# Moving the expert-weight loads of a transformer layer to the last two pairs of each attention step

## The chip, the core and the metric

The kernel runs on one core of a Trainium2 chip. The metric is the device time of one execution in microseconds (us). TensorE (PE) multiplies, VectorE (DVE) and ScalarE (ACT) do element-wise work, GpSimd (POOL) does some of it too and issues DMAs through the software queue, SyncE (SP) only issues DMAs through a hardware queue. Every DMA, whoever issues it, runs on the same 16 DMA engines.

## The reference

The input is 32 sequences of 256 tokens, 128 features each, all in float32. Each token is normalised, and the layer adds three things: the token, an attention block with its own MLP, and a mixture of 9 experts of which every token takes 2.

```python
x = L0_attn_hidden_states
xn = _layernorm(x, axis=-1)
x = x + _L0_attn_ref(xn, ...) + _L0_ffn_ref(xn, Wr, Wg, Wu, Wd)

# attention: 16 heads of 8, causal
attn = softmax(where(causal, Q K^T * scale, -1e9));  ctx = attn @ V
h = xn + ctx @ out_U @ out_V + out_b
h + gelu(_layernorm(h) @ fc1_U @ fc1_V + fc1_b) @ fc2_U @ fc2_V + fc2_b

# experts: E = 9, two per token, inner width 352
hidden = silu(xf @ Wg[e]) * (xf @ Wu[e]);  out = sum over e of cw[t, e] * hidden @ Wd[e]
```

## The kernel before, in words

Engines run their own written-out programs and meet at semaphores. The work has four stages: layer norm and routing scores, attention (from about 93 to 612 us), the experts, and the MLP. The change lies in attention alone.

Attention goes over 16 chunks of 512 tokens, one step per chunk, two sequences per chunk. A step has 24 slots, 12 for each sequence. In each slot PE makes one block of scores (`score_unit`, lines L1022 and L1023), ACT takes its exponential (L817), and PE multiplies by V two slots later. Interleaved with it runs a second pass that is 8 slots or more ahead: `max_unit` (L999, L1002) makes the scores for the row maxima, DVE takes the maxima (L1393), PE turns them (L1053), ACT negates them (`copy_max`, L810), and SP copies the resulting 16x256 numbers, 16 KB, as one more row into the stacked queries with a DMA (`stack_max`, L474). This row is called **the maxima row** here. The score block of slot 0 and that of slot 12 wait for it (`max_stacked`), since the exponential must be taken of scores less their maximum. The row for a step's first sequence is issued near slot 21 of the step before, the row for its second sequence near slot 9.

SP also copies the projected queries into the stack (`stack_q`, L451), 12 DMAs of 32 KB per sequence, the first of them at a step's start and after slot 12. POOL copies the keys (`stack_k_part`, L609, 128 KB each), scatters token rows to their expert slots (`scatter`, L652, 64 KB each), and loads the expert weights (`load_weights`, L600 and L604).

POOL walks a step in 12 **pairs** of slots. At the head of pair k it waits until 2k+1 score blocks of the step are done. Then it issues what the tables put there: scatters at pairs 0 to 8 in steps 3 to 10 (at all 12 pairs in steps 11 to 14), key copies for the next chunk's second sequence at pairs 1, 2 and 3, the bias at pair 7, key copies for the chunk after it at pairs 8, 9 and 10. The zero fills of the slot buffer (`fill`, L589, 516 KB each) are at pairs 0 to 7 in steps 0 and 1, with one more in step 2.

The weights come in 15 loads in steps 3 to 10. Their order is, for each group of three experts, Wg, Wu (528 KB each), then three parts of Wd (192, 192 and 144 KB). They are waited for only in the last step (`experts_loaded`). Before the change a step issues its two loads at pair 0 and pair 6. Within a pair the load is the last thing that POOL issues.

Step 3 begins at about 207 us in the trace and a step takes some 31 to 33 us.

Of the kernel before, what the change touches and what calls it, by code (L numbers as in the profile page):

```python
# [63 lines left out]
def layer_kernel(nc, x_in, w, out):  # L64
# [28 lines left out]
    with whole:  # L93
        ident = keep("ident", [P, P])
        wq = keep("wq", [P, P])
        wk = keep("wk", [P, P])
        wv = keep("wv", [P, P])
        wo = keep("wo", [P, P])
        w1 = keep("w1", [P, HID])
        w2 = keep("w2", [P, HCH, P])  # L100
        q_bias = keep("q_bias", [P, 1])
        k_bias = keep("k_bias", [P, 1])
        v_bias = keep("v_bias", [P, P])
        mlp_bias = keep("mlp_bias", [P, HCH])
        out_bias = keep("out_bias", [P, P])
        fc2_bias = keep("fc2_bias", [P, P])
        with nc.sbuf_tensor("first_words", [P, EXPERTS * (2 * FF + len(FF_CHUNKS) * P)], F32) as first_words:
            pass
        w_gate_up = keep("w_gate_up", [P, EXPERTS, 2 * FF], F32R)
        w_down = keep("w_down", [P, EXPERTS, len(FF_CHUNKS), P])  # L110

        even_stack = keep("even_stack", [P, GROUPS * LANES * CHUNK], F32R)
        assert EXPERTS * 2 * FF <= GROUPS * LANES * CHUNK
        w_hi = even_stack[:, 0:EXPERTS * 2 * FF].rearrange("p (e f) -> p e f", e=EXPERTS)
        mix = keep("mix", [P, tiles, 2])
        slot_of = keep("slot_of", [P, tiles * 2], U32)
        tile_expert = keep("tile_expert", [1, slot_tiles], I32)
        ln2_stats = keep("ln2_stats", [P, tiles * 6])

        first_and_attention(nc, locals())  # L120
        experts_and_mlp(nc, locals())
# [34 lines left out]
def first_and_attention(nc, env):  # L156
# [13 lines left out]
    UNITS = 12  # L170
# [4 lines left out]
    with ExitStack() as stack:  # L175
# [171 lines left out]
        LATE = 3  # L347
        W_STEPS, LAST_ROWS = 8, 8
# [4 lines left out]
        def when(j):  # L353

            step = max(k for k, n in ROWS_AT.items() if n <= j)
            return step, j - ROWS_AT[step]

        XS_AT = {(LATE - 1, 1): 0, (LATE - 1, 2): 1}
        for c in range(2, chunks):
            step, row = when(2 * TPC * (c - 1) - 1)  # L360
# [19 lines left out]

        def weights_at(step, pair):

            if pair in W_AT and LATE <= step < LATE + W_STEPS:
                k = 2 * (step - LATE) + W_AT.index(pair)
                return k if k < W_LOADS else None
            return None

        K_SECOND_AT, K_FIRST_AT, BIAS_AT, W_AT = (1, 2, 3), (8, 9, 10), 7, (0, 6)

        MAX_FROM = 8  # L390
        EARLY = 2 * UNITS - MAX_FROM
# [16 lines left out]
        with nc.Block() as block:  # L408
# [140 lines left out]
            def _(pool):  # L549
# [109 lines left out]
                def step(half, d):  # L659
                    p = at(half, d)  # L660
                    x = p.index
                    last = x == last_chunk
                    two_ahead = x < last_chunk - 1
                    for pair in range(HALVES):
                        after_scores(p, 2 * pair + 1)
                        rows, blank_part, weights = scatter_at(x, pair), fill_at(x, pair), weights_at(x, pair)
                        if x == LATE and pair == 0:
                            pool.wait_ge(slots_ready, 1)
                            pool.wait_ge(zero_filled, 16 * FILLS)
                            pool.wait_ge(routed_all, 1)  # L670
                        if rows is not None:
                            if rows[1] == 0:
                                number_rows(at(0, rows[0]))
                            scatter(at(0, rows[0]), rows[1])
                        if blank_part is not None:
                            fill(blank_part)
                        if pair == BIAS_AT:
                            add_bias(p)
                        if pair in K_SECOND_AT and not last:
                            stack_k_part(at(half, d + 1), 1, K_SECOND_AT.index(pair))  # L680
                        if pair in K_FIRST_AT and two_ahead:
                            if pair == K_FIRST_AT[0]:
                                pool.wait_ge(k_split, x + 3)
                                pool.sem_inc(k_stack_started, 1)
                            stack_k_part(at(half, d + 2), 0, K_FIRST_AT.index(pair))
                        if weights is not None:
                            load_weights(weights)
# [1357 lines left out]
```

## Time and profile before

| | us |
|---|---|
| median of 3 runs | 1030.56 |
| lowest, highest | 1028.12, 1031.29 |
| the profiled execution | 1028.12 |
| its span, first to last instruction | 1026.4 |
| PE busy | 966.4 (94%) |
| DVE busy | 703.0 (68%) |
| ACT busy | 538.1 (52%) |
| POOL busy | 431.6 (42%) |

The span is what the trace covers; 1.7 us lie around it. TensorE's granted clock over the whole run is 0.960 of full speed, and 1.00 in the attention steps 3 to 15. PE is busy nearly all of the attention stage.

### The profile page before, as it was taken

Reading aid. Unit: us, or ns where it says so; the run is one execution under the profiler, and the core shown is the slowest. Engines: PE = TensorE matmul, PEld = TensorE weight load, DVE = VectorE, ACT = ScalarE, POOL = GpSimd, SP = SyncE. Lnnn points to the kernel's source line nnn. Section 1 sums busy time; section 2 is a strip of 40 time slices with the busy share of each in tenths; the row PEclk is TensorE's granted clock in tenths of the full one; section 3 lists DMA queues with packets and bytes.
Section 4 is the critical chain, followed back from the end, with each engine's and each line's share of the span. In section 5 each row is a group of like instructions: output and inputs, shape, how many; then the busy total and the mean of one; then the engine's idle time right before and its main releaser. Section 6 shows DMA issues by size and latency. Waiting matters only on the chain. (4 is left out here: it accounts for less than half of the span.)

```text
span 1026.4 us, 25266 instructions
## 1 busy us (share of the span) xinstructions
PE 966.4 (94%) x7701; PEld 750.1 (73%) x7701; DVE 703.0 (68%) x3192; ACT 538.1 (52%) x1256; POOL 431.6 (42%) x563
## 2 busy tenths in 40 slices
PE   3768999999999999999999987999999999999997
PEld 3435565666666666666666647999999999999896
DVE  4758488877778777787777763555555554558887
ACT  1653255554555555555555574555555555564442
POOL 9462122154544545445555522545445444441110
PEclk9666699999999999999999998999999999999999
DMA  8285355355445455343433204222222222238784
GB/s 234 87 228 177 111 176 185 107 153 127 124 132 154 136 140 143 98 137 114 142 110 117 83 31 121 63 66 63 64 66 69 68 66 61 74 98 252 210 234 134
DMA packets 133558, 127.13 MB, mean 124 GB/s; under 512 B 17274, under 2 KB 113652, under 8 KB 133428
## 3 DMA queue, kind: packets, MB, share of 16 engines
q1 hardware_dynamic: 109860, 67.83, 24.2%
q0 software_dynamic: 20592, 56.43, 17.5%
q10 hardware_dynamic: 2976, 1.26, 0.5%
q8 instruction: 67, 1.10, 0.5%
q14 instruction: 63, 0.52, 0.2%
HBM read 57.15 MB, written 42.60 MB: 97 GB/s over the span
## 5 line engine op out<-in xcount | busy, mean ns | idle before, releaser
L1393 DVE CUSTOM_DVE_ANT_0 att_masked_st<-att_m_ps,att_mask_st 128x128 bf16<-128x128 f32 (+1 forms) x1024 | 313.0, 353 | 109.8 <-PE att_m_ps L999 78.8
L817 ACT ACTIVATE att_probs<-att_t_ps 128x512 f32<-128x512 f32 x384 | 229.4, 598 | 213.2 <-PE att_t_ps L1023 208.6
L1641 POOL DMA_INDIRECT y_scratch<-moe_y,moe_row_now x136 | 132.3, 972 | 151.9 <-DVE moe_y L1895 110.4
L652 POOL DMA_INDIRECT slot_x<-att_xs,att_slot_now x128 | 126.9, 991 | 160.7 <-PE att_t_ps L1023 138.0
L1889 DVE TENSOR_TENSOR moe_hidden<-moe_gate,moe_up_ps 128x352 f32<-128x352 f32 x136 | 70.9, 521 | 113.7 <-ACT moe_gate L1816 110.2
L1023 PE MATMUL att_t_ps<-att_mask_ts,att_ident_b 128*128 128x256 bf16 (+1 forms) x384 | 124.6, 324 | 0.0
L1718 PE MATMUL moe_y_ps<-w_down,moe_hidden_t 128*128 (+1 forms) x816 | 113.8, 275 | 1.3 <-DVE moe_y L1895 1.2
L1816 ACT ACTIVATE moe_gate<-moe_gate_ps 128x352 f32<-128x352 f32 x136 | 63.1, 464 | 96.2 <-PE moe_up_ps L1701 96.2
L1718 PEld LDWEIGHTS moe_y_ps<-w_down,moe_hidden_t 128*128 128x128 f32 (+1 forms) x816 | 101.8, 191 | 2.4 <-issue 2.3
L1393 DVE DVE_READ_ACCUMULATOR2_ANT att_row_max<- 128x1 f32 x1024 | 84.6, 83 | 0.0
L1022 PE MATMUL att_t_ps<-att_odd_stack,att_k_stack 97*128 97x512 f32 x192 | 81.0, 423 | 3.1 <-DMA att_odd_stack<-att_neg_max 2.7
L1022 PE MATMUL att_t_ps<-even_stack,att_k_stack 97*128 97x512 f32 x192 | 82.0, 427 | 1.5 <-DMA even_stack<-att_neg_max 1.3
L1038 PE MATMUL att_pv_ps<-att_probs,att_v_ones 128*32 128x256 f32 x1024 | 82.7, 395 | 0.0
L1023 PEld LDWEIGHTS att_t_ps<-att_mask_ts,att_ident_b 128*128 128x128 bf16 x384 | 37.7, 98 | 61.4 <-issue 49.3
L609 POOL DMA_DIRECT2D att_k_stack<-att_qk_parts x96 | 55.2, 576 | 48.3 <-PE att_t_ps L1023 45.5
L999 PE MATMUL att_m_ps<-att_k_stack,even_stack 96*128 96x256 f32 x256 | 70.6, 359 | 2.4 <-DVE att_row_max L1393 2.3
L999 PE MATMUL att_m_ps<-att_k_stack,att_odd_stack 96*128 96x256 f32 x256 | 68.6, 350 | 0.0
L1710 PE MATMUL moe_hidden_ps<-ident,moe_hidden 128*128 128x128 f32 (+1 forms) x408 | 66.9, 273 | 0.0
L999 PEld LDWEIGHTS att_m_ps<-att_k_stack,even_stack 96*128 96x128 f32 x256 | 42.4, 203 | 22.9 <-issue 18.1
L1701 PE MATMUL moe_gate_ps<-even_stack,moe_x_lo 128*128 x136 | 55.8, 411 | 0.6 <-DVE moe_x_lo L1883 0.6
L999 PEld LDWEIGHTS att_m_ps<-att_k_stack,att_odd_stack 96*128 96x128 f32 x256 | 40.7, 194 | 20.4 <-issue 18.9
L1810 ACT CAST moe_x_hi<-moe_x_ps 128x128 fp32r<-128x128 f32 x136 | 36.2, 266 | 34.0 <-PE moe_x_ps L1682 32.4
(264 smaller groups left out, 2072.9 us busy)
## 6 DMA issues: line engine op xcount, KB each, us to landing
att_k_stack<-att_qk_parts POOLq DMA_DIRECT2D x96, 128.0 KB, 3.2
slot_x<-att_xs POOLq DMA_DIRECT2D x17, 516.0 KB, 3.3
moe_x<-slot_x SPq DMA_DIRECT2D x34, 258.0 KB, 2.8
att_xs<-xn_scratch SPq DMA_DIRECT2D x32, 256.0 KB
mlp_rows<-y_scratch POOLq DMA_DIRECT2D x16, 512.0 KB, 5.4
even_stack<-att_qk_parts SPq DMA_DIRECT2D x192, 32.0 KB
att_odd_stack<-att_qk_parts SPq DMA_DIRECT2D x192, 32.0 KB
xn_scratch<-att_probs POOLq DMA_DIRECT2D x16, 256.0 KB, 3.0
```

Source lines behind the costliest of these rows:

```text
L652: pool.indirect_dma_start(env["slot_x"][:], bass.IndirectOffsetOnAxis(ap=slot_now[c.parity][:, col:col + 1], axis=0), xs[c.parity][:, t, k ...
L817: act.activation(probs[:, m % PT, :], t_ps[m % 2][:], ACT.Exp).then_inc(exp_done, 1)
L999: last = pe.matmul(ps[:, n * SEQ:(n + 1) * SEQ], q[0:ROWS, g, i, hi:hi + P], k[0:ROWS, g, lo:lo + SEQ], start=True, stop=True)
L1022: pe.matmul(by_lane, keys, q[rows, g, lanes, queries], start=True, stop=False, skip_group_check=True)
L1023: pe.matmul(by_lane[:, :, 0:P], ident_b[:], mask_ts[:, lanes, :], start=False, stop=True, skip_group_check=True).then_inc(scores_done, 1)
L1038: last = pe.matmul(pv_ps[b][32 * i:32 * i + 32, at_col:at_col + SEQ], v_ones[c.parity][:, 2 * b, head_of(u, i), :], pt, start=(u == 0), st ...
L1393: last = dve.tensor_tensor_reduce(out=masked_st[m % 2][:, part], in0=m_ps[m % 2][:, part], in1=mask_st[:, SEQ - width:], scale=1.0, scalar ...
L1641: pool.indirect_dma_start(env["y_dram"][:], bass.IndirectOffsetOnAxis(ap=row_now[q.parity][:, t:t + 1], axis=0), y[c.parity][:], None).the ...
L1710: last = pe.transpose(hidden_ps[0:n, k * P:(k + 1) * P], hidden[c.parity][:, col:col + n], ident[:])
L1718: last = pe.matmul(y_ps[:, 0:P], hidden_t[c.parity][0:n, k * P:(k + 1) * P], down_cols[0:n, ds(e * (NCH * P) + k * P, P)], start=(k == 0), ...
L1816: act.activation(gate[c.parity][:], gate_ps[c.parity][:, 0:FF], ACT.Silu).then_inc(gate_done, 1)
L1889: dve.tensor_tensor(hidden[c.parity][:], gate[c.parity][:], up_ps[c.parity][:, 0:FF], ALU.mult).then_inc(hidden_done, 1)
```

## The change

The two weight loads of a step leave pairs 0 and 6 and go to pairs 10 and 11, the last two. Which load belongs to which step stays as it was.

```diff
         def weights_at(step, pair):
 
-            if pair in W_AT and LATE <= step < LATE + W_STEPS:
-                k = 2 * (step - LATE) + W_AT.index(pair)
+            if pair >= UNITS - 2 and LATE <= step < LATE + W_STEPS:
+                k = 2 * (step - LATE) + pair - (UNITS - 2)
                 return k if k < W_LOADS else None
             return None
 
-        K_SECOND_AT, K_FIRST_AT, BIAS_AT, W_AT = (1, 2, 3), (8, 9, 10), 7, (0, 6)
+        K_SECOND_AT, K_FIRST_AT, BIAS_AT = (1, 2, 3), (8, 9, 10), 7
```

`UNITS` is 12, `LATE` is 3, `W_STEPS` is 8 and `W_LOADS` is 15. The programs of PE, DVE, ACT and SP are the same, row for row; only POOL's changes.

POOL at pair 6 to pair 10 of step 3, before. The names: `att_scores_done` is the wait at a pair's head, L652 are scatters, L609 key copies.

```order
L652 DMA slot_x<-att_xs0,att_slot_now0 17408x129 [waits att_scores_done] x3
L600 DMA w_gate_up<-in_L0_ffn_Wu 128x3x352
L652 DMA slot_x<-att_xs0,att_slot_now0 17408x129 [waits att_scores_done]
L637 TENSOR_TENSOR att_xn_both<-att_xn_both,out_bias 128x512 [waits att_xn_loaded1]
L643 COPY att_slot_now1<-slot_of 128x8 [waits att_scores_done]
L644 COPY att_xs1<-att_row_of 128x8
L652 DMA slot_x<-att_xs1,att_slot_now1 17408x129 [waits att_xs_loaded1,att_slot_ready]
L609 DMA att_k_stack1<-att_qk_parts 32x4x256 [waits att_k_split]
L609 DMA att_k_stack1<-att_qk_parts 32x4x256 [waits att_scores_done] x2
L652 DMA slot_x<-att_xs1,att_slot_now1 17408x129 [waits att_scores_done]
L604 DMA w_down<-in_L0_ffn_Wd 128x3x128
```

The Wu load stands at pair 6, ahead of pair 7's scatter; the last two rows are pair 0 of step 4, with the next load.

POOL at pairs 4 to 11 of step 3 and the start of step 4, after.

```order
L652 DMA slot_x<-att_xs0,att_slot_now0 17408x129 [waits att_scores_done] x4
L637 TENSOR_TENSOR att_xn_both<-att_xn_both,out_bias 128x512 [waits att_xn_loaded1]
L643 COPY att_slot_now1<-slot_of 128x8 [waits att_scores_done]
L644 COPY att_xs1<-att_row_of 128x8
L652 DMA slot_x<-att_xs1,att_slot_now1 17408x129 [waits att_xs_loaded1,att_slot_ready]
L609 DMA att_k_stack1<-att_qk_parts 32x4x256 [waits att_k_split]
L609 DMA att_k_stack1<-att_qk_parts 32x4x256 [waits att_scores_done] x2
L600 DMA w_gate_up<-in_L0_ffn_Wg 128x3x352
L600 DMA w_gate_up<-in_L0_ffn_Wu 128x3x352 [waits att_scores_done]
L652 DMA slot_x<-att_xs1,att_slot_now1 17408x129 [waits att_scores_done] x2
L609 DMA att_k_stack1<-att_qk_parts 32x4x256
```

Both loads of the step now stand between the third key copy of pair 10 and the scatter of the next step's pair 0: Wg directly behind that key copy, Wu behind the wait of pair 11.

SP around the same boundary, the same before and after.

```order
L451 DMA att_odd_stack<-att_qk_parts 8x4x256 [waits att_scores_done,att_q_split]
L451 DMA att_odd_stack<-att_qk_parts 8x4x256 x11
L474 DMA even_stack<-att_neg_max 1x16x256 [waits att_max_copied]
L451 DMA att_odd_stack<-att_qk_parts 8x4x256 [waits att_scores_done,att_q_split]
L451 DMA att_odd_stack<-att_qk_parts 8x4x256 x11
```

Nothing moved here; the maxima row (L474) of the next step's first sequence stands between two groups of query copies.

## Rows read from the trace of the kernel before

**Rows 1.** Waits of PE, 205 to 460 us: us in total, times, longest us.

```profile
PE att_t_ps L1022 <- DMA even_stack<-att_neg_max: 1.1, 3, 0.7
PE att_t_ps L1022 <- DMA att_odd_stack<-att_neg_max: 0.6, 2, 0.4
```

**Rows 2.** Windows, steps 3 to 10: us, busy us per engine, PEclk, DMA share, GB/s.

```profile
207.60:460.30 252.70, 250.92 (x2211) 162.19 (x2209) 195.03 (x1138) 142.04 (x256) 124.60 (x161) 1.00 0.49 134
```

**Rows 3.** Timeline of SP and PE, end of step 5: start us, us, instruction.

```profile
300.78 0.55 SPq L474 DMA_DIRECT2D even_stack<-att_neg_max  x1
...
302.71 0.50 PE L999 MATMUL att_m_ps<-att_k_stack,even_stack 96*128 96x256 f32 x2
303.05 0.40 PE L1022 MATMUL att_t_ps<-even_stack,att_k_stack 97*128 97x512 f32 x1
```

**Rows 4.** Line L474, all 32: issue start to landing, min/median/max us.

```profile
DMA to landing us min/median/max: 2.1/2.1/3.3
```

**Rows 5.** DMA view, 301.90 to 302.30 us: queue, packets, MB, share of 16 engines.

```profile
q1 hardware_dynamic: 32, 0.02, 16.4%
```

**Rows 6.** Timeline of SP and PE, end of step 3; landing of that maxima row.

```profile
237.17 0.56 SPq L474 DMA_DIRECT2D even_stack<-att_neg_max  x1
...
239.10 0.50 PE L999 MATMUL att_m_ps<-att_k_stack,even_stack 96*128 96x256 f32 x2
240.29 0.50 PE L1022 MATMUL att_t_ps<-even_stack,att_k_stack 97*128 97x512 f32 x1 [0.69 <-DMA even_stack<-att_neg_max]
...
DMA to landing us min/median/max: 3.1/3.1/3.1
```

**Rows 7.** Timeline of POOL: third key copy of step 5; Wu, Wd; pair 11 (step 11).

```profile
299.13 0.55 POOL L609 DMA_DIRECT2D att_k_stack<-att_qk_parts  x1 [2.33 <-PE att_t_ps L1023]
...
225.75 0.81 POOL L600 DMA_DIRECT2D w_gate_up<-in_L_ffn_Wu  x1
258.24 0.80 POOL L604 DMA_DIRECT2D w_down<-in_L_ffn_Wd  x1
383.62 0.80 POOL L600 DMA_DIRECT2D w_gate_up<-in_L_ffn_Wu  x1
...
490.19 0.99 POOL L652 DMA_INDIRECT slot_x<-att_xs,att_slot_now  x1 [0.93 <-PE att_t_ps L1023]
```

**Rows 8.** Timeline of SP: four groups of query copies, then the row after step 11.

```profile
226.72 8.94 SPq L451 DMA_DIRECT2D att_odd_stack<-att_qk_parts  x12
259.22 8.56 SPq L451 DMA_DIRECT2D even_stack<-att_qk_parts  x12
384.62 5.70 SPq L451 DMA_DIRECT2D even_stack<-att_qk_parts  x8
447.58 8.83 SPq L451 DMA_DIRECT2D even_stack<-att_qk_parts  x12
489.12 0.55 SPq L474 DMA_DIRECT2D even_stack<-att_neg_max  x1
```

**Rows 9.** DMA view, 448.89 to 449.79 us, beside no weight load.

```profile
q1 hardware_dynamic: 66, 0.06, 19.1%
```

**Rows 10.** DMA view, 226.90 to 228.95 us, beside the Wu load of step 3.

```profile
DMA packets 104, 0.44 MB, mean 214 GB/s; under 512 B 0, under 2 KB 0, under 8 KB 104
q0 software_dynamic: 104, 0.44, 80.4%
```

**Rows 11.** DMA view, 384.70 to 386.95 us, beside the Wu load of step 8.

```profile
DMA packets 97, 0.38 MB, mean 171 GB/s; under 512 B 6, under 2 KB 6, under 8 KB 97
q0 software_dynamic: 97, 0.38, 79.3%
```

**Rows 12.** DMA view, 260.53 to 261.43 us, behind the Wd load of step 4.

```profile
q1 hardware_dynamic: 69, 0.06, 20.0%
q0 software_dynamic: 13, 0.00, 1.9%
```

**Rows 13.** DMA view, 306.80 to 308.70 us: issues, us to landing beside a weight load.

```profile
att_k_stack<-att_qk_parts POOLq DMA_DIRECT2D x1, 128.0 KB, 4.6
```

**Rows 14.** Page, DMA issues: the same copies over the whole run.

```profile
att_k_stack<-att_qk_parts POOLq DMA_DIRECT2D x96, 128.0 KB, 3.2
```

**Rows 15.** Line L474, one row each: landing at the ends of steps 8, 11 and 12.

```profile
DMA to landing us min/median/max: 2.6/2.6/2.6
DMA to landing us min/median/max: 2.5/2.5/2.5
DMA to landing us min/median/max: 3.3/3.3/3.3
```

## The prediction

> **What bounds the kernel now.** I read the waits of PE first. Over the steps that load weights, 205 to 460 us, PE waits for one thing only: the maxima row, five times, 1.7 us in all [rows 1]. The windows then say that PE is busy 250.92 of 252.70 us there, at full granted clock [rows 2]. So in these steps PE is the bound. Work on POOL costs nothing unless it makes PE wait, and the only door it could come through is the maxima row, because it is the one thing PE already waits for.
>
> Next I read how much room that row has. At the end of step 5 SP issues it at 300.78, and the score block that needs it starts at 303.05, 2.27 us later, 0.34 us behind the start of PE's last matmul before it [rows 3]: PE did not wait. The landing is 2.1 us after the issue in most of the 32 cases [rows 4]. The room is 2.27 - 2.1, about 0.17 us. At the end of step 3 the landing took 3.1 us instead, the distance between the same two matmuls was 1.19 us instead of 0.34, and PE lost 0.85 us [rows 6]. A late landing above 0.17 us goes one to one into PE's time, and since PE is the bound, into the end. Its data packets run between 1.1 and 1.5 us after the issue [rows 5].
>
> **The change part by part.** It adds and removes no instruction; 15 loads of 0.8 us issue time move on POOL.
>
> What it removes. At pair 0 and pair 6 the loads stood behind the start of slots 0 and 12, that is behind the blocks that need the maxima row, while the rows themselves are issued near slots 9 and 21. They were as far from the next row as they can be. What they hold up there are scatters and query copies, which nobody waits for (no other line stands in rows 1). So taking them away gives 0. If the cover is wrong, the ceiling is all of PE's waiting in these steps by rows 1, 1.7 us.
>
> What it adds at pair 10. There the load stands behind the third key copy. In step 5 that copy starts at 299.13 and takes 0.55 [rows 7], so the load would be issued from 299.68, 1.10 us before the maxima row. The maxima row is issued 0.3 us after POOL has finished issuing the load, and its packets come due at +1.2, in the middle of the load's transfer.
>
> What a load does to SP's packets at such a distance is in the trace, since the query copies at pair 6 stand almost the same. Beside no load, a group begun at 447.58 has 66 packets of queue q1 (SP's) between 1.31 and 2.21 us after its issue [rows 8, 9]. Beside the Wu load (528 KB) of step 3, issued at 225.75, the group begins at 226.72 [rows 7, 8], and from 226.90 to 228.95 only q0 (POOL's queue) has packets: 104, and none of q1 [rows 10]. At the Wu load of step 8, issued at 383.62, q1 has again nothing from 384.70 to 386.95, although a group began at 384.62 [rows 7, 8, 11]. So a 528 KB load keeps q1 out until 3.2 to 3.3 us after its own issue. For the maxima row that is 3.2 - 1.1 = +2.1 to 3.3 - 1.1 = +2.2 instead of +1.2: 0.9 to 1.0 us late. Less the room of 0.17 that is 0.75 to 0.85; I take 0.9, as the 16 packets will not all come at the first chance.
>
> A 192 KB load (Wd) acts otherwise. It was issued at 258.24, the group of queries at 259.22, and in the same stretch after the issue, 260.53 to 261.43, q1 has 69 packets, as many as beside no load [rows 7, 8, 12]. With the third key copy directly ahead of it in the queue I give it 0.1 us each.
>
> By the order of loads, pair 10 gets Wg in steps 3 and 8, Wu in step 6, and a part of Wd in steps 4, 5, 7, 9 and 10: 3 heavy, 5 light. The ends of steps 3 and 8 are already late, landings of 3.1 and 2.6 us [rows 6, 15]. If the causes overlap, a heavy load adds only the rest, 0.1 and 0.6; if they add, 0.9 each. I take 0.5 and 0.7. Step 6 has no late landing and pays 0.9 in full.
>
> Sum: 0.5 + 0.9 + 0.7 + 5 x 0.1 = 2.6 us.
>
> The bounds of a heavy one: below, 0 (its packets slip between). Above, the key copy issued beside a load at about 307, which landed after 4.6 us where the median is 3.2 [rows 13, 14]: 1.4 late, 1.2 of cost. Three of these are 3.6 us. For a light one: below 0; above, the nearest rows are the ends of steps 11 and 12, where a 64 KB scatter stands at pair 10: landings of 2.5 and 3.3 [rows 15], 0.4 and 1.2 late, 0.2 and 1.0 of cost. I stay near 0.1, since there the scatter pushes the key copy itself to the maxima row's issue, and here the key copy keeps its place. At 0.5 each five would cost 2.5.
>
> What it adds at pair 11. The wait at its head ends about 1.07 us after the maxima row's issue (490.19 against 489.12 [rows 7, 8]), so this load is issued from +1.1 to +1.9 and holds q1 from about +2.2 to +4.3, when a punctual row has landed. What it holds up are query copies and scatters of the next step, with many slots to go: 0. Behind the load on POOL stands pair 0's scatter, whose own wait ends later.
>
> **A rule weighed.** The rows show q1 without a packet for 2.0 and 2.2 us beside 528 KB loads [rows 10, 11]. The Trainium skill, DMA: Bandwidth & Descriptors, section Queues, rings and completion order, says that each DMA engine goes round robin between the queues it has work for, one packet at a time. By that rule the maxima row would wait for about one packet on each engine and the change would cost next to nothing. The trace does not agree for SP's queue beside these loads, so I keep that as a rival and do not forecast by it.
>
> **The rivals.**
>
> 1. No delay. A maxima row of 16 KB finds its turn between the load's packets. One packet of a load takes 0.804 x 16 x 2.05 / 104 = 0.25 us [rows 10], so it is at most 0.25 late, 0.08 of cost, and three make 0.25 us: 1030.8. For it: the row is one small packet per engine. Against it: rows 10 and 11. The rule of the Trainium skill named above would give this time.
>
> 2. Slower beyond doubt. The row does not get through between the two loads either. At the ends of steps 3 and 8 both loads are 528 KB. If q1 stays shut until the second one is through, that is 1.1 + 3.2 = +4.3 instead of +1.2, 3.1 late and 2.9 of cost, twice, less the 0.85 and 0.3 paid today: 4.7. With step 6 (0.9) and the light ones (0.5) it is +6.1: 1036.7. It decides when the second load's descriptors reach an engine before the row's packet has gone. For it: the second load is issued at +1.1, before the held packet is free at +2.1. Against: the row's packet was queued first. The light loads at their upper value instead (2.1 + 2.5 = 4.6) give 1035.2.
>
> 3. Faster. Some of the late landings of today are set off by where POOL's stream stands, and go away with it. Ceiling: the 1.7 us of rows 1, with no delay added: 1028.9.
>
> **How the numbers follow.** The profiled execution took 1028.12 us, 1026.4 of span and 1.7 around it; with the change it would be 1030.7. It was the fastest of three, 2.44 under the median. I forecast the median, 1030.56 + 2.6 = 1033.2. A measurement of this kernel can tell about 0.3% from no change, 3.1 us. Chances: forecast 0.52, rival 1 0.13, rival 2 0.28, rival 3 0.07. The forecast's own spread is 0.5 to 4.5 us, and about 0.14 of its 0.52 lies above 3.1. So slower 0.28 + 0.14 = 0.42, faster beyond 0.3% 0.05 (rival 3 mostly stays inside), within it 0.53. The range leaves out little of rivals 1 and 3 and the far end of rival 2: 1029.8 to 1037.5.
>
> **What would show it.** In the profile after: landings of L474 at the ends of steps 3, 6 and 8 of 3.0 us or more, and about 2.1 to 2.3 at the ends of 4, 5, 7, 9 and 10; PE's waits for the maxima row up from 1.7 to 4 or 5 us over these steps; q1 without packets while the pair 10 load runs; steps 0 to 2 and 11 to 15 unchanged, and the expert and MLP stages too. I am wrong if the three landings stay near 2.1, if a wait of PE on another line appears, or if the light loads cost as much as the heavy ones.

## The result, and the profile after

The changed kernel is slower: 1042.34 us median (1041.32 to 1045.42) against 1030.92 us for the kernel before, measured beside it, each the median of 4 executions. The ratio is 1.0107, 95% interval 1.0069 to 1.0146, some 11 us. I had forecast 1033.2 us and a range that ended at 1037.5. The place was right and the size was wrong by a factor of four: 2.6 us more were forecast, some 11 came.

The page of the changed kernel; its profiled execution took 1045.36 us.

```profile
span 1043.6 us, 25266 instructions
PE 975.9 (94%) x7701; PEld 756.9 (73%) x7701; DVE 702.6 (67%) x3192; ACT 538.1 (52%) x1256; POOL 431.4 (41%) x563
```

The instructions are the same in number, but PE is busy 975.9 us instead of 966.4. The same matmuls took longer, which is the first thing that I had not reckoned with.

The windows view of the changed kernel, from the first score block of step 3 to that of step 11 (us, then busy us of PE, PEld, DVE, ACT, POOL, then PEclk, DMA share, GB/s):

```profile
209.87:473.23 263.36, 254.72 (x2211) 164.42 (x2209) 195.29 (x1141) 142.02 (x256) 123.76 (x161) 0.99 0.46 130
```

It answers to [rows 2]. The stretch takes 10.7 us more, 263.36 against 252.70. Length less PE's busy time is its idle time: 8.6 us, where it was 1.8. So 6.9 us of the loss is waiting, and the other 3.8 us is PE being busy longer with the same work. This one row separates the two terms, and I use it for every kernel below.

PE's waits in the same stretch (us in total, times, longest us), answering to [rows 1]:

```profile
PE att_t_ps L1022 <- DMA att_odd_stack<-att_neg_max: 4.5, 4, 1.6
PE att_t_ps L1022 <- DMA even_stack<-att_neg_max: 4.1, 3, 1.9
```

PE still waits for the maxima row and for nothing else. The timelines of POOL, SP and PE at the end of step 3, answering to [rows 6, 7]:

```profile
237.43 0.55 POOL L609 DMA_DIRECT2D att_k_stack<-att_qk_parts  x1 [1.58 <-PE att_t_ps L1023]
237.97 0.78 POOL L600 DMA_DIRECT2D w_gate_up<-in_L_ffn_Wg  x1
239.95 0.77 POOL L600 DMA_DIRECT2D w_gate_up<-in_L_ffn_Wu  x1 [1.21 <-PE att_t_ps L1023]
...
239.06 0.56 SPq L474 DMA_DIRECT2D even_stack<-att_neg_max  x1
...
241.00 0.50 PE L999 MATMUL att_m_ps<-att_k_stack,even_stack 96*128 96x256 f32 x2
243.22 0.49 PE L1022 MATMUL att_t_ps<-even_stack,att_k_stack 97*128 97x512 f32 x1 [1.73 <-DMA even_stack<-att_neg_max]
```

The loads stand where the prediction put them, the first 1.09 us ahead of the row, the second 0.89 us behind its issue. The score block starts 4.16 us after the row's issue, where it was 3.12 before and is 2.27 when nothing is late. The DMA view from 239.50 to 241.30 us shows the hold:

```profile
DMA packets 103, 0.45 MB, mean 248 GB/s; under 512 B 0, under 2 KB 0, under 8 KB 102
q0 software_dynamic: 102, 0.43, 86.7%
q8 instruction: 1, 0.02, 3.7%
```

For 1.8 us no packet of SP's queue q1 ran, although the row's were due at about 240.3. The row q8 is a fetch of 16 KB of instructions, which also runs on one of the DMA engines.

At the end of step 6 the second term shows as well. PE's timeline of the changed kernel, and the windows of the two stretches behind the ends of steps 6 and 7:

```profile
337.59 0.50 PE L999 MATMUL att_m_ps<-att_k_stack,att_odd_stack 96*128 96x256 f32 x2
339.69 0.50 PE L1022 MATMUL att_t_ps<-att_odd_stack,att_k_stack 97*128 97x512 f32 x1 [1.60 <-DMA att_odd_stack<-att_neg_max]
...
342.85 1.90 PE L982 MATMUL att_free_ps<-wv,att_xt 128*128 128x128 f32 x8
```

```profile
341.18:344.60 3.42, 3.42 (x25) 2.74 (x18) 1.12 (x7) 0.97 (x2) 1.71 (x2) 0.50 0.18 58
375.31:378.72 3.41, 3.41 (x26) 2.14 (x25) 1.43 (x7) 1.28 (x3) 1.03 (x1) 0.50 0.19 63
```

PE stood idle for 1.60 and 1.93 us at these two ends. 1.5 and 0.7 us after it had resumed, its granted clock went to 0.50, the lower of its two levels, for 3.4 us each time, while PE was fully busy. Half of 6.8 us is 3.4 us, which is nearly all of the 3.8 us of longer work. The kernel before has 1.00 in the whole stretch [rows 2].

The ends of the steps together, from both traces. "Start" is the time from the row's issue to the start of the score block that needs it:

| end of step | load at pair 10 | start before | start after | more |
|---|---|---|---|---|
| 3 | Wg, 528 KB | 3.12 | 4.16 | 1.04 |
| 4 | Wd, 192 KB | 2.28 | 3.18 | 0.90 |
| 5 | Wd, 144 KB | 2.27 | 2.27 | 0 |
| 6 | Wu, 528 KB | 2.28 | 4.05 | 1.77 |
| 7 | Wd, 192 KB | 2.67 | 4.36 | 1.69 |
| 8 | Wg, 528 KB | 2.61 | 3.99 | 1.38 |
| 9 | Wd, 192 KB | 2.27 | 2.37 | 0.10 |
| 10 | Wd, 144 KB | 2.28 | 3.05 | 0.77 |

The sum is 7.65 us. The rows at slot 12 of these steps were 0.4 us less late than before, and the clock costs 3.4 us: 7.65 - 0.4 + 3.4 = 10.65, against 10.7 measured.

The profiled execution lost 17.2 us against that of the kernel before, not 10.7. The first score block of all started 3.0 us later, before anything that changed, and the experts and the MLP took some 4 us more; both stages run partly at the lower clock in either kernel, for stretches that differ from one execution to the next. The medians differ by 11.4 us, so I hold the changed steps alone against the ratio.

### The profile page after: what moved, and what is told of

The parts are those of the page before. It is cut to its first block and busy times, and to the rows that moved or that the text cites. A ratio compares the mean times of both kernels' runs of the same rounds, so it can differ in the third digit from the quotient of the medians.

```text
span 1043.6 us, 25266 instructions
## 1 busy us (share of the span) xinstructions
PE 975.9 (94%) x7701; PEld 756.9 (73%) x7701; DVE 702.6 (67%) x3192; ACT 538.1 (52%) x1256; POOL 431.4 (41%) x563
## 3 DMA queue, kind: packets, MB, share of 16 engines
q0 software_dynamic: 20592, 56.43, 17.2%
## 5 line engine op out<-in xcount | busy, mean ns | idle before, releaser
L652 POOL DMA_INDIRECT slot_x<-att_xs,att_slot_now x128 | 125.8, 983 | 159.3 <-PE att_t_ps L1023 134.9
L1022 PE MATMUL att_t_ps<-att_odd_stack,att_k_stack 97*128 97x512 f32 x192 | 81.4, 425 | 6.8 <-DMA att_odd_stack<-att_neg_max 6.2
L1022 PE MATMUL att_t_ps<-even_stack,att_k_stack 97*128 97x512 f32 x192 | 82.9, 432 | 4.3 <-DMA even_stack<-att_neg_max 4.1
L609 POOL DMA_DIRECT2D att_k_stack<-att_qk_parts x96 | 56.2, 586 | 49.7 <-PE att_t_ps L1023 47.4
```

The costliest lines, as they stand in the source:

```text
L652: pool.indirect_dma_start(env["slot_x"][:], bass.IndirectOffsetOnAxis(ap=slot_now[c.parity][:, col:col + 1], axis=0), xs[c.parity][:, t, k ...
L1022: pe.matmul(by_lane, keys, q[rows, g, lanes, queries], start=True, stop=False, skip_group_check=True)
```

## The experiments

The kernel before was timed beside each of them. The ratio is taken from 4 to 12 executions of each changed kernel. Length, idle and busy time are steps 3 to 10 of one profiled execution, from the windows view; idle is length less PE's busy time. That stretch also moves from one execution to the next: g2_one is 3.5 us longer than the kernel before, its one moved load accounts for 1.5 of them, and 1.6 are later rows at slot 12, where no load was moved. So a difference of 2 us in the length says little by itself.

| kernel | ratio, 95% interval | length | PE idle | PE busy |
|---|---|---|---|---|
| before | | 252.70 | 1.8 | 250.92 |
| changed | 1.0107, 1.0069 to 1.0146 | 263.36 | 8.6 | 254.72 |
| e1_ten | 1.0132, 1.0078 to 1.0186 | 270.22 | 9.7 | 260.55 |
| e2_eleven | 1.0007, 0.9986 to 1.0029 | 253.72 | 3.5 | 250.26 |
| e4_light | 1.0020, 0.9988 to 1.0052 | 256.19 | 5.5 | 250.67 |
| e5_heavy | 1.0115, 1.0059 to 1.0170 | 263.38 | 8.5 | 254.83 |
| f1_long | 1.0047, 1.0026 to 1.0069 | 256.83 | 6.6 | 250.28 |
| f1_short | 1.0037, 1.0009 to 1.0064 | 255.72 | 4.6 | 251.12 |
| f2_busy | 1.0072, 1.0050 to 1.0095 | 262.37 | 6.2 | 256.19 |
| f3_nine | 1.0120, 1.0056 to 1.0183 | 263.42 | 9.4 | 254.00 |
| g1_longer | 1.0111, 1.0083 to 1.0139 | 266.38 | 8.8 | 257.60 |
| g2_one | 1.0009, 0.9986 to 1.0031 | 256.21 | 4.8 | 251.41 |
| g3_rows | 0.9991, 0.9975 to 1.0007 | 251.67 | 1.3 | 250.37 |
| g4_rows_keys | 0.9957, 0.9939 to 0.9975 | 251.18 | 1.2 | 250.03 |

**Which load does it.** The first load of each step at pair 10 and the second at pair 6 (e1_ten), and the first at pair 0 and the second at pair 11 (e2_eleven). The names behind # are labels of mine, here and below:

```diff
-        K_SECOND_AT, K_FIRST_AT, BIAS_AT, W_AT = (1, 2, 3), (8, 9, 10), 7, (0, 6)
+        K_SECOND_AT, K_FIRST_AT, BIAS_AT, W_AT = (1, 2, 3), (8, 9, 10), 7, (10, 6)   # e1_ten
+        K_SECOND_AT, K_FIRST_AT, BIAS_AT, W_AT = (1, 2, 3), (8, 9, 10), 7, (0, 11)   # e2_eleven
```

> The first load of each step stays at pair 10, as in the changed kernel; the second goes back to pair 6. Theory A (the load at pair 10 alone holds the maxima row up, the one at pair 11 is innocent): PE's waits for L474 in steps 3 to 10 stay at 7 to 9 us as in the changed kernel, and the time at 8 to 11 us over the kernel before. Theory B (the pair 10 load holds the row until about 3.2 us after its own issue, as forecast, and the load at pair 11 keeps the queue shut beyond that): waits fall to 3 to 5 us, landings at the ends of steps 3, 6 and 8 to 3.0 to 3.2 us, and the time to 2 to 4 us over before, with no drop of the clock. Theory C (the load at pair 11 does it alone): waits of 1.7 us, no difference.

> The second load of each step stays at pair 11, the first goes back to pair 0. Theories A and B: the row has landed before this load's packets begin, so PE's waits stay near 1.7 us and the time within 1 us of the kernel before. Theory C: waits of 5 us or more and 5 to 10 us over before.

With the load at pair 10 alone the whole loss is there; with the load at pair 11 alone there is none that can be measured. Theory A holds, B and C fall. At the end of step 3 of e1_ten PE stood idle for 2.69 us, and its windows behind the ends of steps 3 and 6 are:

```profile
243.20:250.00 6.80, 6.11 (x35) 4.55 (x36) 1.55 (x8) 1.79 (x3) 1.80 (x2) 0.50 0.38 105
342.10:348.90 6.80, 6.53 (x37) 4.97 (x37) 1.55 (x8) 1.79 (x3) 2.21 (x3) 0.50 0.17 56
```

There are four drops in steps 3 to 10, three of 6.8 us and one of 3.4, 23.9 us in all. They are what lengthens this profile against that of the changed kernel although its rows are hardly later: idle is 1.0 us more, PE's busy time 5.8 us. Whether the kernel as such is slower than the changed one the intervals do not tell, 1.0078 to 1.0186 against 1.0069 to 1.0146.

**Heavy or light.** Only the Wd loads at pairs 10 and 11, the 528 KB ones at 0 and 6 (e4_light), and the reverse (e5_heavy):

```diff
-            if pair in W_AT and LATE <= step < LATE + W_STEPS:
-                k = 2 * (step - LATE) + W_AT.index(pair)
-                return k if k < W_LOADS else None
+            for late, at_pairs in ((False, W_AT), (True, (UNITS - 2, UNITS - 1))):
+                if pair in at_pairs and LATE <= step < LATE + W_STEPS:
+                    k = 2 * (step - LATE) + at_pairs.index(pair)
+                    if k < W_LOADS and (k % W_PARTS >= 2) == late:     # e4_light; e5_heavy has < 2
+                        return k
```

> Only the nine Wd loads (192 and 144 KB) are at pairs 10 and 11, the six of 528 KB are at pairs 0 and 6. By the prediction's term for light loads (0.1 us each): 0.5 us over before. By what the changed kernel's ends of steps 4, 7 and 10 show (PE starts 3.18, 4.36 and 3.05 us after the issue of L474 instead of 2.28): 2.5 to 4 us over before, and a drop of the clock behind step 7 worth 1.7 us more.

> Only the six loads of 528 KB are at pairs 10 and 11, the nine Wd loads are at pairs 0 and 6. If heavy and light loads act apart, this and the light kernel share the 10.6 us that the changed kernel loses in steps 3 to 10: 5 to 7 us over before here, with one drop of the clock (behind step 6 or 8), landings of 3.7 us or more at the ends of steps 3, 6 and 8. If at the end of step 6 the Wd load at pair 11 was needed for the 4.05 us there, that end falls to 3.0 to 3.3 us here.

The light loads lose 3.5 us in their steps, seven times the 0.5 us of the prediction, with no drop of the clock behind step 7 this time; some 2.6 of the 3.5 lie at the ends of steps 7 and 10, where the start is 4.00 and 3.60 us after the row's issue. Their ratio does not tell them from no change. The price of a light load is not steady: with the same 144 KB load at pair 10 of step 10 the start is 2.28 us in e1_ten, 3.05 in the changed kernel and 3.60 here. The heavy ones lose 10.7 us, as much as the changed kernel, 6.8 of it waiting and 3.9 longer work in two drops. At the end of step 6 the start is 4.26 us here with the Wd load back at pair 6, so the load behind it was not needed. At the end of step 8 PE was idle longer than at either of the ends that had a drop in the changed kernel, and the clock kept its level:

```profile
405.71 0.51 PE L1024 MATMUL att_t_ps<-att_odd_stack,att_k_stack 97*128 97x512 f32 x1 [1.90 <-DMA att_odd_stack<-att_neg_max]
```

**Is the clock a cause of its own?** SP issues small DMAs of 512 B ahead of the maxima row, and the loads stay where they were. Each kernel has one of the three HOLD rows; left out are the scratch tensor, the counter `held` and the wait for `held_back` at the end.

```diff
+                HOLD = {(6, 0): 5, (10, 0): 5}                      # f1_long
+                HOLD = {(c, 0): 2 for c in (5, 6, 7, 10, 11)}       # f1_short
+                HOLD = {(6, 0): 10, (10, 0): 10}                    # g1_longer
                 def stack_max(c, b):
                     sp.wait_ge(max_copied, 2 * c.index + b + 1)
+                    for _ in range(HOLD.get((c.index, b), 0)):
+                        sp.dma_start(hold_dram[held[0]:held[0] + 1, :], ident[0:1, :]).then_inc(held_back, 16)
+                        held[0] += 1
```

> The kernel before, with its loads where they were. SP issues five small DMAs of 512 B ahead of the maxima row at the ends of steps 5 and 9, so that the row is late with no load near it. Theory A2 (a long wait of PE costs more than itself, because the granted clock falls to half behind it, as the changed kernel shows at 341 and 375 us): PE waits about 2 us or more at each of the two, the clock falls behind at least one, and steps 3 to 10 take 4.5 us of waits plus 1.7 to 3.4 us for each drop. Theory B2 (the drops belong to the loads, not to the waits): the waits alone, 4 to 5 us, and no drop.

> The kernel before, with two such small DMAs ahead of the maxima row at the ends of steps 4, 5, 6, 9 and 10: ten in all as in the run beside it, but each wait under 1 us. Theory A2: waits of 4 to 5 us in total and no drop of the clock, so it is faster than the run with two long waits by the drops. Theory B2: the same time as that run.

Five small DMAs took SP 1.42 us, less than I had assumed, so the long waits were not long: 1.2 us each. No drop came in either kernel, and both lost waiting time alone. That pair was inconclusive, and I ran the kernel with ten.

> As the run with five small DMAs ahead of the maxima row at the ends of steps 5 and 9, where PE stood idle 1.2 us each time and the clock kept its level, but with ten, 2.8 us of SP's time. Nothing about the loads is changed. If a longer stand of PE is what lets the clock fall, PE waits about 2.6 us at each of the two ends and the granted clock drops to half behind at least one of them, for 3.4 us or more; steps 3 to 10 then take 5.3 us of waits plus 1.7 us or more for each drop. If drops belong to the loads, 5.3 us and no drop.

The timelines of SP and PE at the end of step 5 in g1_longer (its line numbers are 8 or 9 higher), then its windows behind the two ends:

```profile
303.51 2.90 SPq L480 DMA_DIRECT2D hold_scratch<-ident  x10
306.45 0.56 SPq L482 DMA_DIRECT2D even_stack<-att_neg_max  x1
...
305.44 0.50 PE L1008 MATMUL att_m_ps<-att_k_stack,even_stack 96*128 96x256 f32 x2
308.63 0.80 PE L1031 MATMUL att_t_ps<-even_stack,att_k_stack 97*128 97x512 f32 x1 [2.68 <-DMA even_stack<-att_neg_max]
...
312.96 1.92 PE L991 MATMUL att_free_ps<-wv,att_xt 128*128 128x128 f32 x8
```

```profile
308.22:315.02 6.80, 6.39 (x36) 4.83 (x37) 1.55 (x8) 1.79 (x3) 2.84 (x4) 0.50 0.42 116
441.33:448.10 6.77, 5.93 (x35) 4.37 (x35) 1.56 (x8) 1.79 (x3) 2.06 (x4) 0.50 0.25 76
```

There is no load near the row, PE stood idle 2.7 us at each of the two ends, and each time the clock was at half for 6.8 us; it had fallen before PE resumed, as the first matmul of 0.80 us shows. Idle rose by 7.0 us, 5.4 of them at these two ends, and PE's busy time by 6.7 us. The drop belongs to PE's standing idle and needs no load, and it costs as much again as the wait.

The other side of the test fills the wait. f2_busy is e1_ten with four matmuls whose result is overwritten, ahead of the wait at the starts of steps 4, 7, 8 and 9. The wait for `exp_done`, which tells that the buffer they write is free, moves ahead of them and of the wait for the row; PE waited for both before either way.

```diff
+                    if not (isinstance(c.index, int) and c.index == 0 and m < 2):
+                        pe.wait_ge(exp_done, 2 * UNITS * c.index + m - 1)
+                    if m == 0 and c.index in (4, 7, 8, 9):
+                        for _ in range(4):
+                            pe.matmul(ps[:].rearrange("p (i s) -> p i s", s=SEQ), k[0:ROWS, 0, lo:hi], q[0:ROWS, 0, 0:2, lo:end],
+                                      start=True, stop=True, skip_group_check=True)
                     if u == 0:
                         pe.wait_ge(max_stacked[b], 16 * (c.index + 1))
-                    if not (isinstance(c.index, int) and c.index == 0 and m < 2):
-                        pe.wait_ge(exp_done, 2 * UNITS * c.index + m - 1)
```

> The kernel with the first load at pair 10 and the second at pair 6, and in addition four matmuls whose result is thrown away, 1.6 us, ahead of the wait for the maxima row at the starts of steps 4, 7, 8 and 9. If the drops of the clock (24 us at half clock in that kernel's profile) come from PE standing idle, they go or shrink: the waits shown fall from 8.6 to about 3 us, the rows land when they did, and the time falls by 5 to 10 us against the kernel without those matmuls. If the drops come from elsewhere, the time stays within 1 us or rises.

PE at the end of step 3 in f2_busy, answering to the 2.69 us idle of e1_ten:

```profile
240.35 1.10 PE L1015 MATMUL att_t_ps<-even_stack,att_k_stack 96*128 96x512 f32 x4
242.86 0.50 PE L1026 MATMUL att_t_ps<-even_stack,att_k_stack 97*128 97x512 f32 x1 [1.40 <-DMA even_stack<-att_neg_max]
```

Work that nobody needs made the kernel faster: steps 3 to 10 took 262.37 us instead of 270.22, and the medians are 1040.5 against 1048.2 us. The two were not timed together and their intervals touch, but the slowest of the 7 executions of f2_busy, 1044.07 us, lies below the fastest of the 4 of e1_ten, 1045.87. The score block at the end of step 3 still started 4.8 us after the row's issue. One drop of 3.4 us was left of the four, behind these 1.40 us of idle time.

**How long a load holds the row.** f3_nine has the first load at pair 9 (`W_AT = (9, 6)`). g2_one moves one single load, the Wg of step 5, to pair 10, at an end without an instruction fetch:

```diff
-            if pair in W_AT and LATE <= step < LATE + W_STEPS:
-                k = 2 * (step - LATE) + W_AT.index(pair)
+            at_pairs = (0, UNITS - 2) if step == 5 else W_AT
+            if pair in at_pairs and LATE <= step < LATE + W_STEPS:
+                k = 2 * (step - LATE) + at_pairs.index(pair)
```

> The first load of each step at pair 9, one pair earlier than in the changed kernel, the second at pair 6. It is issued about 4 us before the maxima row, and a load shuts SP's queue for about 3.3 us after its issue. Theory A (the hold is the load's own transfer on the 16 engines): no wait beyond the kernel before, time within 1 us of it. If the loads harmed by anything that lasts longer (the key copy of pair 10 queued behind the load, which then meets the row), 3 us or more.

> The kernel before with one 528 KB load (Wg) moved from pair 6 to pair 10, in step 5 alone, whose end has no instruction fetch beside it and no late row. By the prediction's term for one heavy load PE starts 3.1 to 3.2 us after the row's issue instead of 2.28, 0.9 us lost, no drop. By what the changed kernel and its parts show at the ends of steps 3, 6 and 8 (4.0 to 5.1 us) it starts after 4.0 us or more, 1.8 us lost, with or without a drop of the clock worth 1.7 to 3.4 us. In between would say that the instruction fetch at the other ends is a part of the price.

POOL, SP and PE at the end of step 3 in f3_nine:

```profile
236.81 0.76 POOL L600 DMA_DIRECT2D w_gate_up<-in_L_ffn_Wg  x1
237.93 0.57 POOL L609 DMA_DIRECT2D att_k_stack<-att_qk_parts  x1 [0.36 <-issue]
...
239.58 0.56 SPq L474 DMA_DIRECT2D even_stack<-att_neg_max  x1
...
244.57 0.50 PE L1022 MATMUL att_t_ps<-even_stack,att_k_stack 97*128 97x512 f32 x1 [2.56 <-DMA even_stack<-att_neg_max]
```

The load stands 2.8 us ahead of the row, and the score block starts 5.0 us after it. The DMA view from 239.60 to 241.10 us has POOL's queue alone:

```profile
q0 software_dynamic: 108, 0.42, 90.3%
```

So 2.8 us of distance did not save the row. In the packet records of the trace the load itself was still running, until 241.1 us, 4.3 us after its issue; the packets of the third key copy, now behind it in POOL's queue, run from 240.8 to 242.1. What each of the two cost is not shown apart. The time came out as the expectation's second branch had it, 12 us over before, but the load alone outlasted the 3.3 us that the first branch gave it. The same end in g2_one's clean place, in POOL's, SP's and PE's timelines (line numbers one higher), then the DMA view from 304.10 to 305.80 and from 305.80 to 306.80 us:

```profile
302.90 0.77 POOL L601 DMA_DIRECT2D w_gate_up<-in_L_ffn_Wg  x1
304.00 0.55 SPq L475 DMA_DIRECT2D even_stack<-att_neg_max  x1
...
305.93 0.50 PE L1000 MATMUL att_m_ps<-att_k_stack,even_stack 96*128 96x256 f32 x2
307.79 0.50 PE L1023 MATMUL att_t_ps<-even_stack,att_k_stack 97*128 97x512 f32 x1 [1.35 <-DMA even_stack<-att_neg_max]
```

```profile
q0 software_dynamic: 92, 0.38, 84.0%
...
q0 software_dynamic: 54, 0.16, 40.5%
q1 hardware_dynamic: 32, 0.02, 6.2%
```

This is the prediction's case to the tenth of a microsecond: the load is issued 1.10 us ahead of the row. Up to 1.8 us after its issue the row has no packet. Its 32 packets (16 of data, 16 of the semaphore) then come one by one within the next 1.0 us, where undisturbed they take 0.4 us [rows 5]. The packet records say what each of them waited for: every one of the 16 data packets starts within 0.01 us behind a semaphore packet of the load, and the load has one such packet on each engine, as its last. So on each engine the row went behind the whole of the load's share, eight packets of 4224 B. The records do not name the engines; this is read from the times, 16 of 16. The score block starts at 3.79 instead of 2.27 us: one heavy load costs 1.5 us, without a fetch and without a drop of the clock. The ratio of the kernel does not tell that from no change; the profile does.

**A version that beats both.** The loads stay at pairs 0 and 6. Ten scatters in every step from 3 to 14 (g3_rows), so that pairs 10 and 11 carry none, and with it the key copies at pairs 7, 8 and 9 (g4_rows_keys):

```diff
-        ROWS_OF = {step: 9 if step < LATE + W_STEPS else 12 for step in range(LATE, chunks - 1)} | {chunks - 1: LAST_ROWS}
+        ROWS_OF = {step: 10 for step in range(LATE, chunks - 1)} | {chunks - 1: LAST_ROWS}
-        K_SECOND_AT, K_FIRST_AT, BIAS_AT, W_AT = (1, 2, 3), (8, 9, 10), 7, (0, 6)
+        K_SECOND_AT, K_FIRST_AT, BIAS_AT, W_AT = (1, 2, 3), (7, 8, 9), 7, (0, 6)      # g4_rows_keys only
```

> The kernel before with ten scatters in each of steps 3 to 14 instead of nine in steps 3 to 10 and twelve in 11 to 14, so that no scatter is issued at pairs 10 and 11. The rows at the ends of steps 11 to 14 (PE starts 2.52, 3.36, 2.67 and 2.42 us after the issue) should come nearer to 2.28: up to 1.8 us less, 1 us expected. If the instruction fetch alone makes them late, nothing changes.

> As the run with ten scatters per step, and the three key copies for the chunk after the next at pairs 7, 8 and 9 instead of 8, 9 and 10, so that POOL issues nothing at pairs 10 and 11. If whatever POOL's queue carries beside the row makes it late, the ends of steps 3, 7 and 8 (3.12, 2.67 and 2.61 us) improve as well, 2 to 3 us less than the kernel before in all; if the fetch of instructions does it alone, the same as the kernel before within 1 us. A wait of POOL for the keys at pair 7 would show as new idle time on POOL and cost nothing.

The waits of PE in g4_rows_keys over all of steps 3 to 14, and its windows for steps 3 to 10 and 11 to 14:

```profile
PE att_t_ps L1022 <- DMA even_stack<-att_neg_max: 0.9, 2, 0.7
PE att_t_ps L1022 <- DMA att_odd_stack<-att_neg_max: 0.2, 1, 0.2
```

```profile
210.18:461.36 251.18, 250.03 (x2211) 161.96 (x2209) 194.61 (x1137) 141.81 (x256) 133.41 (x171) 1.00 0.49 139
461.36:585.11 123.75, 123.74 (x1103) 80.38 (x1101) 95.86 (x567) 69.44 (x126) 58.69 (x75) 1.00 0.38 111
```

In steps 11 to 14 PE is now idle for 0.01 us. With no scatter at pair 10 the start at the end of step 11 is 2.27 us in both kernels; in the twelve with one there it is 2.51 to 2.63.

At the ends of steps 3, 8, 12 and 13, where an instruction fetch runs, g4_rows_keys has 2.27 to 2.31 us too. That is not shown to come from POOL's silence. The q8 row of the DMA view, from 237.10 to 239.40 us in the kernel before (end of step 3) and from 364.10 to 366.40 us in g4_rows_keys (end of step 7):

```profile
q8 instruction: 1, 0.02, 5.4%
...
q8 instruction: 1, 0.02, 3.2%
```

The first fetch took 1.98 us. By the packet records it began 0.02 us after the row's issue, and the last packet of the row went when it ended, at 1.99 us instead of 1.40: late by 0.6 us, and the landing by 1.0 [rows 6], with nothing of POOL's in the way. The second began at 0.79 us, took 1.17, and the row's last packet went at 1.95 us; there the start is 3.14 us, though POOL issues nothing near. At the four ends where g4_rows_keys is punctual the fetch was over by 1.25 us after the row's issue, when the row's packets run anyway. So a fetch makes the row late by itself when it outlasts the time of the row's packets, and its moment moves without any edit: at the end of step 3 of g2_one, whose program is that of the kernel before up to there, it began at 0.45 us and the start is 3.23.

The ratio is 0.9957, interval 0.9939 to 0.9975, with a median of 1029.53 us against 1033.54 beside it: faster beyond the interval, by 0.4%. g3_rows alone can't be told from the kernel before. In the profiles steps 3 to 14 account for 2.9 us of it, part of which is when the fetches fell; the rest of the 4 us is not placed.

## Why the prediction was wrong, point by point

- *PE is the bound, and the maxima row is the only door.* Right. All new waiting, in every kernel with moved loads, is at the score block (L1022, or its line in that kernel) for that row.
- *Taking the loads from pairs 0 and 6 gives 0.* Not contradicted: e2_eleven vacates pair 6, e1_ten pair 0, and neither shows a gain.
- *A 528 KB load shuts SP's queue until about 3.2 us after its issue.* Near, for the first packet. In g2_one the queue opened 2.9 to 3.0 us after the load's issue, in the changed kernel at step 3 not before 3.3 us.
- *0.9 us for a heavy load.* This step failed by its size. I had counted until the first packet goes. The row is on 16 engines, and it has landed when the last of them has let it through. Clean, it costs 1.5 us (g2_one): the first packet of the row went 0.7 us later than undisturbed (1.9 us after the issue, not 1.2), the last one 1.2 us later (2.6, not 1.4). Beside an instruction fetch or with a late POOL it is 1.0 to 2.1 us on top of what was lost before, in all kernels with one at pair 10. The three together cost 4.2 us in the changed kernel, forecast 2.1.
- *0.1 us for a light load, 0.5 in all.* This failed too: 3.5 us in the changed kernel, 1.7 of them at the end of step 7, more than two of the three heavy loads cost. That light loads cost as much as heavy ones was one of the prediction's own signs of being wrong. The row that I took the 0.1 from [rows 12] shows q1 at its full count at one end of one step. The rows that I had as the upper bound, the ends of steps 11 and 12 [rows 15], were the better guide, at an upper value of 0.5 each and 2.5 us in all.
- *Nothing else.* The missing term is the clock. Of 10.7 us, 3.4 are PE at half clock behind waits of 1.6 and 1.9 us, and g1_longer and f2_busy show it from both sides. No step of the prediction had it. But it is not the whole miss: the 6.9 us of waiting alone lie above the 4.5 us at which the forecast case ended.
- *Rival 1*, no delay, is out: q1 had no packet for 1.8 us. The prediction priced it by the rule on round robin in the Trainium skill, DMA: Bandwidth & Descriptors, section Queues, rings and completion order, with one packet of the trace, 4224 B, as the packet of that rule. The section itself puts a packet at typically some 9 to 17 descriptors. A load's share on one engine is nine rows of the trace, eight of data and one of the semaphore; if these are one packet in the section's sense, its rule gives the wait of g2_one, and what failed is the unit that the prediction took. The changed kernel does not fit that at the end of step 6, where the load was issued only 0.24 us ahead of the row: the row's packets went 2.5 to 2.9 us after its issue, between those of the load, which ran on until 3.4. Which unit holds is not settled here. *Rival 2* had the right sign but not its mechanism: e1_ten loses as much without a second load behind, and so does the end of step 6 in e5_heavy. *Rival 3* is out for this change.

What stays open: why the drop follows an idle time of 1.6 us at one end and not one of 1.7 us at another, both in the changed kernel; why a light load costs nothing at one end and 1.3 us at another; and why PE started 1.1 us after the row's last packet in g2_one where it takes 0.8 us undisturbed. None of them was tried.

## What to carry to other kernels

Cost a late transfer by the last of its engines, not by the first packet that gets through; a small transfer on a critical path wants the stretch ahead of it free of bulk DMAs, though they stand in another engine's queue. Where the bound engine is TensorE, a single wait has a second price that may or may not come: behind waits of 1.4 to 1.9 us the clock was at half for 3.4 or 6.8 us at some ends and not at others here, and behind all of 2.4 us or more it was. Add it to the range before you close it. A bulk load with slack belongs behind the critical transfer, as in the kernel before and at pair 11 of e2_eleven. And where an instruction fetch falls on the transfer, look at several profiles before you credit an edit: at the end of step 3 the six kernels that are alike up to there have 2.79 to 3.23 us from issue to start.

## What the runs showed of the hardware

- A 528 KB load on POOL's queue kept a 16 KB transfer of SP's queue without a packet for 1.8 us after that transfer's issue in g2_one. Each of its 16 data packets then went within 0.01 us of the end of the load's share on one DMA engine.
- A fetch of 16 KB of instructions held one packet of such a transfer until it ended: 1.99 us after the issue in the kernel before (end of step 3), 1.95 us in g4_rows_keys (end of step 7), where undisturbed the last one goes at 1.40 us.
- PE's clock was at half for 3.4 us behind idle times of 1.60 and 1.93 us in the changed kernel and of 1.45 us in f3_nine, and for 6.8 us behind 1.87 us in e1_ten and 2.68 us in g1_longer. It stayed at full level behind 1.22 us in f1_long, 1.35 us in g2_one, 1.54 and 1.73 us in the changed kernel, 1.57 us in e4_light and 1.90 us in e5_heavy.
- Matmuls without use, 1.1 us at each of four waits, won 7.8 us in steps 3 to 10, between one profile of e1_ten and one of f2_busy.
